# The last edge stream multiplies its partial sums in two f32r parts instead of one f32 product

## The reference, cut to what matters

```
h = (xn @ W).reshape(N, 8, 32)
e = leaky_relu(a_src[src] + a_dst[dst], 0.2)
ee = exp(e - emax[dst])
denom = segment_sum(ee, dst)
msg = h[src] * (ee / denom[dst])[:, :, None]
out = segment_sum(msg, dst) + xn @ W_res + bias
out = layer_norm(out);  out = out + gelu(out @ w1 + b1) @ w2 + b2      # then the fourth layer:
y = sum over 8 experts of share[e] * (relu(bn(relu(bn(x @ W1[e])) @ W2[e])) @ Wo[e] + bo[e])
```

## Time and profile before

| | us |
|---|---|
| median of three runs | 3200.69 |
| the profiled execution, its own time | 3199.64 |
| its span, first to last instruction | 3198.0 |
| PE busy | 2751.4 (86%) |
| DVE busy | 2169.6 (68%) |
| POOL busy | 1738.8 (54%) |
| ACT busy | 1531.7 (48%) |
| mean granted TensorE clock | 0.931 |

### The profile page before, as it was taken

How to read it: one execution, slowest core, us unless ns; L and a number is a source line. 1 busy time by engine, 2 the same in 40 slices (tenths; PEclk the granted TensorE clock), 3 DMA queues, 4 the chain that set the end, 5 groups by cost and what they waited for, 6 DMA issues and landing times.

```text
span 3198.0 us, 51615 instructions
## 1 busy us (share of the span) xinstructions
PE 2751.4 (86%) x17241; PEld 2450.5 (77%) x17241; DVE 2169.6 (68%) x5133; ACT 1531.7 (48%) x2928; POOL 1738.8 (54%) x1691
## 2 busy tenths in 40 slices
PE   8468888888899865846799999999999999999998
PEld 7347777777687655836789788887988888798887
DVE  9635655555555566647677878878787787877654
ACT  6113333333333233523456566566666666666665
POOL 0477777777777716557655555455554455544100
PEclk9989999999999887956789999999999999999999
DMA  3666666666666611677787767677676777767534
GB/s 101 184 182 199 192 191 191 180 196 198 183 201 194 187 47 48 224 188 212 236 249 222 240 207 245 219 223 241 206 251 208 233 236 215 250 204 226 160 118 139
DMA packets 369271, 625.87 MB, mean 196 GB/s; under 512 B 86045, under 2 KB 237599, under 8 KB 368995
## 3 DMA queue, kind: packets, MB, share of 16 engines
q1 hardware_dynamic: 290659, 407.24, 40.1%
q0 software_dynamic: 75168, 211.78, 23.3%
q10 hardware_dynamic: 3168, 3.42, 0.3%
HBM read 508.86 MB, written 113.37 MB: 195 GB/s over the span
## 4 chain that ended last, share of the span: by engine, by line
PE 35%; DVE 12%; issue 5%; ACT 4%; POOL 3%; DMA 1%; SPq 0%; DVEq 0%; ACTq 0%
PE PB L116 27%; POOL G L2091 3%; DVE G L2433 2%; DVE WGl L2439 2%; PE PB L2147 2%; PE PB L2120 2%; PE PB L2122 2%; DVE XR L2601 1%; PE PB L2135 1%; DVE H1l L2589 1%; DMA RI<-resd 1%; PE PB L2182 1%; DVE AR L2471 1%; ACT WGh L2285 1%; ACT TFm L2358 0%
## 5 line engine op out<-in xcount | busy, mean ns | idle before, releaser
L2091 POOL DMA_INDIRECT G<-tab,SRCL x784 | 871.2, 1111 | 744.3 <-DVE WGl L2439 529.5
L899 POOL DMA_INDIRECT G<-tab,SRCL x782 | 768.8, 983 | 263.4 <-issue 245.5
L2358 ACT ACTIVATE TFm<-PB,BIA,SCL 128x512 f32<-128x512 f32 (+1 forms) x416 | 312.5, 751 | 286.0 <-PE PB L116 267.6
L931 PE MATMUL PB<-G,OR 128*128 128x257 f32 x782 | 265.3, 423 | 119.1 <-DMA G<-tab,SRCL 97.3
L116 PE MATMUL PB<-H1h,MW 128*128 128x512 f32 (+1 forms) x832 | 301.8, 404 | 29.9 <-DVE H1l L2589 20.9
L2285 ACT CAST WGh<-G 128x1056 fp32r<-128x1056 f32 x196 | 210.3, 1073 | 238.4 <-DVE G L2433 237.4
L116 PE MATMUL PB<-MW,H2h 128*128 128x256 f32 x1568 | 300.7, 289 | 16.1 <-DVE H2l L2589 15.4
L116 PE MATMUL PB<-YTMh,MW 128*128 128x512 f32 (+1 forms) x832 | 286.7, 394 | 6.7 <-ACT TF L2323 6.7
L116 PEld LDWEIGHTS PB<-MW,H2h 128*128 128x128 f32 x1568 | 246.9, 192 | 25.3 <-DVE H2l L2589 18.8
L2120 PE MATMUL PB<-WGh,OR 128*128 128x264 f32 x784 | 227.4, 316 | 39.7 <-DVE WGl L2439 39.2
L931 PEld LDWEIGHTS PB<-G,OR 128*128 128x128 f32 x782 | 136.2, 206 | 162.1 <-DMA G<-tab,SRCL 133.4
(11 more groups left out here) (345 smaller groups left out, 7706.5 us busy)
## 6 DMA issues: line engine op xcount, KB each, us to landing
MW<-msplit SPq DMA_DIRECT2D x312, 512.0 KB, 4.6
ord<-OR SPq DMA_DIRECT2D x392, 128.0 KB
OR<-ord SPq DMA_DIRECT2D x196, 256.0 KB, 4.3
ROW<-relrow SPq DMA_DIRECT2D x196, 128.0 KB
G<-tab,SRCL POOLq DMA_INDIRECT x1566
msplit<-FWs SPq DMA_DIRECT2D x68, 256.0 KB, 3.2
tab<-ACC SPq DMA_DIRECT2D x7, 896.0 KB, 7.4
resd<-RSG SPq DMA_DIRECT2D x49, 128.0 KB, 2.4
```

The costliest lines, as they stand in the source:

```text
L899: po.indirect_dma_start(b.G[:, u % RU, q, 0:256], None, c.tab0, bass.IndirectOffsetOnAxis(ap=c.SRCL[:, 2 * u + q:2 * u + q + 1].bitcast(U3 ...
L931: pe.matmul(PB[w % 2][:, 0:257], b.OR[:, u % RH, 0, :], b.G[:, u % RU, 0, :], start=first, stop=False)
L2091: po.indirect_dma_start(b.G[:, j % RP, u, :], None, c.tab1, bass.IndirectOffsetOnAxis(ap=c.SRCL[:, 4 * j + u:4 * j + u + 1].bitcast(U32), ...
L2358: a.activation(b.TM[:, m, 0:n], PB[of][:, 0:n], ACT.Relu, bias=b.BIA[:, l, q:q + 1], scale=b.SCL[:, l, q:q + 1]).then_inc(relu, 1)
```

## The change

- ACT's copy of a window becomes a rounding to f32r, `WIN[0]`, counted by a new semaphore `win_hi`.
- A new DVE step "evac_lo" reads the window from PSUM bank 2, subtracts the rounded part and writes `WIN[1]`. It counts `evac`, on which PE's next window and "tile" wait. It has a written cost of 0.5 and stands behind the "low" of the unit in which the window ended; steps of other streams can come between them.
- "tile" does two f32r products for each window in place of one f32 product, so 324 in place of 162.
- To make room, the window slots go from 5 (RW) to 4 (RV), `E1` loses its second buffer, `CV` lies in `TM`, and the rows of "rows" go into `YM`; `Yt` is gone. "rows" now waits for the transposes of the experts' rows of the group before, and step 0 of "prepare" for those of the group's own rows.

```
+RV = 4
     [edge_stream]
             if i % 3 == 0 or i == NJ:
                 w = (i - 1) // 3
                 put(("evac", w), 0.3)
+                done_window = [w]
                 waiting.extend(ready_after(w))
 ...
         if i < NJ:
             put(("low", i), 1.2)
+        for w in done_window:
+            put(("evac_lo", w), 0.5)
+        done_window = []
     [last_alloc]
-    b.WIN = sb("WIN2", [P, RW, 264])
-    b.OS = sb("OS2", [P, 4, P])
-    b.E1 = sb("E1", [P, 2, 4, 16])
+    b.WIN = [sb("WIN2h", [P, RV, 264], F32R), sb("WIN2l", [P, RV, 264], F32R)]
+    b.OS = sb("OS2", [P, 4, P], F32R)
+    b.E1 = sb("E1", [P, 4, 16])
-    b.Yt = sb("Yt9", [P, 2, D])
-    b.CV = sb("CV", [P, 10, 16])
+    b.CV = b.TM[:, 1, 256:416].rearrange("p (a n) -> p a n", a=10)
     [last_pe, step "tile"]
             for i, w in enumerate(TW[t]):
-                ins = pe.matmul(PB[1][:, 0:264], b.OS[:, i, :], b.WIN[:, w % RW, :], start=(i == 0), stop=(w == TW[t][-1]))
+                pe.matmul(PB[1][:, 0:264], b.OS[:, i, :], b.WIN[0][:, w % RV, :], start=(i == 0), stop=False)
+                ins = pe.matmul(PB[1][:, 0:264], b.OS[:, i, :], b.WIN[1][:, w % RV, :], start=False, stop=(w == TW[t][-1]))
     [last_act, step "evac"]
-            if w >= RW:
-                on.wait_ge(S.tile_mm, tiles_of(w - RW)[1] + 1)
-            a.copy(b.WIN[:, w % RW, :], PB[2][:, 0:264]).then_inc(S.evac, 1)
+            if w >= RV:
+                on.wait_ge(S.tile_mm, tiles_of(w - RV)[1] + 1)
+            a.copy(b.WIN[0][:, w % RV, :], PB[2][:, 0:264]).then_inc(S.win_hi, 1)
     [last_dve]
+        elif step == "evac_lo":
+            w, = x
+            on.wait_ge(S.win_hi, w + 1)
+            if w >= RV:
+                on.wait_ge(S.tile_mm, tiles_of(w - RV)[1] + 1)
+            v.tensor_tensor(b.WIN[1][:, w % RV, :], PB[2][:, 0:264], b.WIN[0][:, w % RV, :].bitcast(F32),
+                            ALU.subtract).then_inc(S.evac, 1)
     [last_dve, step "rows"]
             if h:
                 on.wait_ge(S.rows_t, h)
+            if LGROUP_OF[LHALVES[h][0]]:
+                on.wait_ge(S.xrows_t, 2 * LGROUP_OF[LHALVES[h][0]])
             for i, k in enumerate(LHALVES[h]):
-                ins = norm(v, b.Yt[:, i, :], AR[:, k % RA, :], k, c.MEAN, c.RSTD)
+                ins = norm(v, b.YM[:, i, :], AR[:, k % RA, :], k, c.MEAN, c.RSTD)
     [last_dve, step "prepare", s == 0]
+                on.wait_ge(S.rows_t, LHALF_OF[tiles[-1]] + 1)
```

## The result

The changed kernel takes 3194.97 us, the median of 11 runs (3189.91 to 3198.26); the kernel before takes 3202.03 us in 11 runs beside it (3194.84 to 3210.84). The ratio is 0.9972, with the interval [0.9963, 0.9981]: about 9 us faster (6 to 12). That is a real gain, but within the 0.5% that the prediction called no change, and some 6 us short of the 14.9 that it summed. The profiled execution took 3191.12 us, span 3189.4 (before: 3199.64 and 3198.0).

The account below looks back on a forecast made before the run. PE was taken as fullest after 1600 us, with DVE near; POOL's gathers led before. From 3199.64 us, 25.4 gained less 7.4 and 3.1 (14.9) gave 3184.7, stated as 3184.5, range 3168 to 3201.

Parts of the forecast that it names:

- no change: Whole kernel: time within 0.5% (16.0 us) of before, given chance 0.48; faster had 0.44, slower 0.08.
- rival B: Last phase: DVE and ACT in fixed order swallow half the products' gain, DVE terms stand; 3197 us, chance 0.22.
- Part 1: PE's tile: two f32r products for one f32 save 32.9 us of PE, 25.4 us of the chain.
- not a whole one: Chain of waits: a microsecond of PE is worth more than one of DVE, neither worth a whole one.
- rival A: After 1600 us PE's time comes through whole and DVE's additions are hidden; 3174 us, chance 0.17.
- Parts 2 and 3: DVE at evac_lo: 27.5 us of subtractions and 11.4 of waits, each charged 27%, cost 7.4 and 3.1 us.
- HT9l (L2521): Sign on PE: it should wait a little more for this DVE step at windows 19, 35 and 51.
- Part 4: Everything else, including slots, YM and the shifted merged list: costs nothing, give or take 4 us.
- The product's 4.7% share: Up to 1600 us: the tile product holds 4.7% of 210 us in the chain, 9.9 us, half of it to go.
- Rival D: Up to 1600 us: shorter tiles idle PE, lowering its clock; 3194 us, chance 0.04, sign a mean below 0.60.
- the third that I had named: Sign of a wrong size: PE's idle time grows by more than a third of what its products lose.
- Rival C: DVE's queue behind evac_lo: PE needs its steps next, so all DVE waiting and work is paid; 3213 us, chance 0.08.

Follow-up runs that it names:

- e11: Kernel before with the new buffer room and two f32r products, low part constant zero, no DVE subtraction, old step order: 0.9921 of before.
- e5: Kernel before with only the new buffer room, steps in the old order, f32 product, no DVE subtraction: 1.0004 of before.
- e1: Kernel before with the new room and step order and two f32r products, low part constant zero, no DVE subtraction: 0.9967 of before.
- e4: Kernel before with the new room and step order only, f32 product and plain copy kept, no DVE subtraction: 1.0024 of before.
- the three changed rows: Profiled executions of the unmodified changed kernel: its first measurement, e7 and e12; timed 0.9972, 1.0001 and 0.9987 of before.
- e2: e4 plus DVE's subtraction and its waits, result unused, still the one f32 product: 1.0037 of before.
- e3: Changed kernel with DVE's subtraction reading constants and waiting for nothing, low part constant zero: 0.9970 of before.
- e6: Changed kernel with evac_lo's written cost at 0, so all other steps keep the old order: 1.0003 of before.
- e7: Changed kernel unmodified, a control on e6's chip: 1.0001 of before.
- e12: Changed kernel unmodified, a control on the chip of e9 to e11: 0.9987 of before.
- e8: e6 with DVE's subtraction moved later, behind the next unit's weights and right ahead of tile and sum: 1.0169 of before.
- e9: Changed kernel with the subtraction on POOL, ACT copying then rounding, and five weight slots instead of six: 0.9981 of before.

## Why the prediction was right and wrong

**Right: direction, range and the likeliest outcome ("no change").** 3195 lies in 3168 to 3201, on the slow side of it. The forecast of 3184.5 is 10.5 us off, and its own range (3178 to 3191) missed by 4 us; rival B's 3197 was nearer. On two other chips the changed kernel's gain isn't clear of noise (1.0001 and 0.9987). From window 17 to the last instruction the sum came out well: it has 17.8 us for the products there and 8.6 for DVE (49 subtractions and nearly all of the waits, at 27%), 9.2 gained; measured are 8.8. That is in part luck, as the next paragraphs show. The miss is ahead of window 17.

**Part 1, the products: right, a little too large.** The pace (0.12), the number of records and the saving of PE (16.2 us in the stretch, of which about 15 show once the clock's loss is taken out: e11 less e5 is 16.7 - 1.8, e1 less e4 13.7 + 1.8) came as worked out. The chain's share forecast 3.2% x 820 x 0.46 = 12.1 us for the stretch; measured are 10.7 and 10.4, two thirds of PE's saving. To the last instruction the two pairs give 16.4 and 16.3, for 17.8 in the sum. So "not a whole one" was right, and rival A is refuted: with no DVE work added at all, idle time takes back 3.2 to 6.0 us (e1, e11).

**Parts 2 and 3, DVE: a price near enough by luck, from the wrong mechanism.** For the stretch the prediction's 27% gives 3.7 us for 13.6 of work, and 2.1 for 7.8 of waiting: 5.8. Against e1 the three changed rows are 5.6, 6.3 and 10.2 us longer. But in this stretch little of it is time that PE waits. The idle time grows by 0.9 to 1.7 us. The rest is the lower clock: 5.0, 5.1 and 10.2 us more lost than in e1. e2 against e4 shows it again without the new products (0.4 idle, 6.8 clock). To the last instruction the three rows are 3.7, 6.7 and 10.3 us longer than e1, with 2.8, 1.9 and 0.9 of idle time and 0.0, 5.1 and 10.3 of the clock, and e3 is 3.8 longer with 4.0 of idle time and 1.6 less of the clock. So idle time takes 1 to 4 us, and the clock anything from nothing to 10; that DVE's work costs is shown, the clock's share of its price is not settled. And the wait at evac_lo, to which I gave 3.1 us of the sum, is free as far as rows can tell: e3 has none and is as long. It was 15.5 us where I had 11.4, in 13 places where I had six (1.43 instead of 2.1 at window 35). PE waits for HT9l (L2521) less than before, 3.2 us for 5.2, where I had a little more.

**Part 4, the order: its sign depends on the rest.** "At nothing, give or take 4 us" holds in the stretch: e4 and e1 are 0.9 and 1.1 us longer than e5 and e11, and with the subtraction the new order is rather the better one, by 0.8 to 5.4 us. From window 17 to the last instruction the new order takes 6.7 (e4) and 6.8 us (e1) more without the subtraction, 4.0 and 1.7 of them idle time of PE. With it the new order takes 3.6 to 10.2 us less than e6, 1.3 to 3.2 of them idle time. So without the subtraction the term was a little over its 4 us, and in the kernel that was forecast the order helped if anything; with the clock's loss varying by 10 us between equal programs, no run settles its size. e4's timed loss of 8 us (1 to 15) against e5's 1 (-8 to 11) is on different chips and settles none either. A trap lies at the end of the edge stream. From the copy of window 61 to that of window 65, e4 takes 3.0 us more than e5, e1 3.6 more than e11, and after 2.1 more than before. But the new order also puts more of PE's work between these two copies (669 records for 658 in e4, 663 for 658 in the other two pairs), so at least part of it is work that has moved and not cost.

**The first 400 us: the largest miss of the sum.** Products were to bring 9.9 x 0.50 + 5.8 x 0.46 = 7.6 us up to 1800; the two kernels are level at window 17. PE's work there did fall: busy time times clock is 86.8 us against 90.6 up to 1600. But PE was at the half level for longer, and POOL's gathers lead the chain as before (40.8%, before 41.1):

```profile
by line: POOL G L2095 40.8%; issue 16.1%; PE PB L117 10.0%; DMA G<-tab,SRCL 5.0%; DMA RI<-resd 3.8%; DMA ROW<-relrow 2.2%; DVE WGl L2443 1.8%; PE PB L2124 1.6%; PE PB L2126 1.5%; DVE G L2437 1.2%; SPq L2013 1.0%; DVE AR L2482 0.8%; PE PB L2
```

The product's 4.7% share was no gain to be had, since the next gather gives the pace. That is my reading of both traces; no run separates it from the clock. It rests on one pair of executions: on the other chips windows 0 to 17 take 387.4 to 390.4 us in the three kernels with the f32 product and 380.4 to 391.2 in six with the new ones (e1, e3, e6, e7, e11, e12), so some gain there isn't excluded.

**Rival D was put in the wrong place.** I looked for the clock up to 1600, and wrote that after 1600 "the clock is 0.98 and has little room". Up to 1600 it did fall, to 0.59 from 0.64, below the 0.60 that I had named as the sign. But no run shows that the products set it: from window 0 to 17 the clock's loss is 92.9 us after and 79.4 before, on the other chips 85.5 to 92.2 without the new products and 89.7 to 96.2 with them. After 1600, in those 2%, is the most of the DVE step's price from window 17 to 49. All seven rows with the subtraction on DVE and within the usual order lose 8.5 to 15.4 us, the five others with it absent 3.4 to 6.9, and POOL's 6.8. To the last instruction the groups overlap: 14.1 to 26.0 with it, 10.8 to 15.7 without. What the DVE step raises in each pair is the number of PE's idle pieces of 1 us or more from window 17 to 49: 16 in e4 and 19 in e2; 19 in e1, 22 in e3, 24 and 25 in the changed kernel (15 before). The clock fell behind only some of them: 4 times before, 3 times in e1, 6 or 7 times in the changed kernel.

The Trainium skill ("TensorE: Matmul & The Clock Gate", Part 1) has the half clock as the state that PE falls back to when it isn't kept busy. The slices behind windows 32 and 38 agree in direction: each fall stands behind 1.8 to 2.3 us of idle PE. They also show that it happens in a stretch in which PE is busy 94% of the time.

**Rival B came half true.** PE's idle time grew by 7.9 us for 16.2 us of products saved, 49%, more than the third that I had named as the mark of a wrong size. That its number was the nearest is luck: it halves the products' gain everywhere, while two thirds were kept behind window 17 and none showed ahead of it. Rival C didn't occur: PE waits 9.7 us for the subtraction, in six places. e8 shows that it was a matter of where the step stands.

**What stays open:** why the same program loses 10 us to the clock in one execution and 15 in another; how the DVE step's price is divided between waiting and the clock; why nothing was gained ahead of window 17 on the first chip; how much of the old order's 819.9 is order; and why e7 and e12 timed closer to before than the changed kernel on its own chip did.

## What to carry to other kernels

When a fast engine is 95% busy beside another at 80%, price work added to the second one by the slices where the first idles behind it. Look at the granted clock in slices of a few us there: a mean of 0.98 hid falls to the half level that in most rows cost more than the waiting did. When two instruction orders are compared between two marks, count the instructions between them first: a moved mark looks like a cost. And when two versions differ by less than 0.5%, split each stretch into busy time, idle time and the clock's loss first; the idle time repeats to within one or two microseconds, the total doesn't.

## What the runs showed of the hardware

- TensorE's clock falls to the half level for about 3.4 us, in places for 10.2, inside a stretch whose mean is 0.98 or 0.99. In all rows but e8 each fall begins within 8 us behind an idle piece of PE of 1.1 to 2.4 us, but most such pieces have no fall behind them. It falls mostly at the same windows (22 in twelve of these thirteen rows, 38 in eleven), and by very different amounts in equal programs.
- A 128x264 subtraction into f32r takes 423 ns on DVE with an operand in PSUM, and 989 ns on POOL out of SBUF (739 to 1818, in e9). ACT's rounding of the same size takes 373 ns from PSUM and 413 ns from SBUF.
- DVE's 32 subtractions from SBUF constants (e3) take the same 424 ns as from PSUM.
- A DVE instruction that overlaps such a subtraction of POOL in time takes longer: with both operands in SBUF, 128x512, 870 to 1035 ns instead of about 684 (e9).
- The kernel before has a median of 3202 us on one chip and of 3429 to 3452 on three others, with most of the difference ahead of the last phase.
